# Mixture by pairs of experts, with rows turned by DMA, in a ViT layer on one core

## The reference

```
hidden = einsum('npd,hd->nph', patches, W_lin) + b_lin;  h = concat([cls, hidden])
q, k, v = heads(layernorm(h) @ qkv_weight.T)              # 12 heads of 16
q = layer_norm(q) * 16**-0.5;  k = layer_norm(k)
h = h + (softmax(q @ k.T) @ v) @ proj_weight.T
y = layernorm(h)                                          # 12608 rows of 192
scores = sigmoid(y @ gate_weight.T)                       # 8 experts
w, idx = top 2 experts of the 2 best groups of 4, by scores + gate_bias; w normalised
out_e = (silu(y @ w1[e].T) * (y @ w3[e].T)) @ w2[e].T     # 128 inner numbers
h = h + sum over idx of w * out_e + shared expert(y)
```

## Time and profile before

| what | us |
|---|---|
| median of 2 runs | 1719.84 (1719.72 to 1719.96) |
| profiled execution, its own time | 1721.13 |
| its span | 1719.3 |
| PE busy | 1622.7 (94%) |
| DVE busy | 1274.5 (74%) |
| ACT busy | 1010.0 (59%) |
| POOL busy | 602.2 (35%) |
| one attention step | 14.19 |
| one full mixture group | 29.69 |

### The profile page before, as it was taken

One profiled execution on the slowest core, in us unless ns is written; L12 is line 12 of the kernel. 1 busy time (PEld: TensorE's weight loads), 2 busy tenths in 40 slices (PEclk: granted clock), 3 DMA queues, 4 the chain that ended last, 5 costly groups with the idle time before them and its releaser, 6 DMA issues. The chain is left out here.

```text
span 1719.3 us, 44326 instructions
## 1 busy us (share of the span) xinstructions
PE 1622.7 (94%) x16914; PEld 1124.4 (65%) x16914; DVE 1274.5 (74%) x3660; ACT 1010.0 (59%) x2089; POOL 602.2 (35%) x658
## 2 busy tenths in 40 slices
PE   5999999999999999999998499999999999999998
PEld 4777777777777777777776255555555555555555
DVE  5677777666666666666664488888888888888887
ACT  2777776666666666666666345445454545455452
POOL 2333333333333333333331143343434343343433
PEclk8999999999999999999999699999999999999999
DMA  7233333333333333333310100001010100001000
GB/s 236 68 76 76 76 76 76 76 77 76 76 76 77 76 77 78 77 78 78 79 35 12 35 29 27 31 19 38 20 38 20 34 24 29 29 20 38 16 20 16
DMA packets 40863, 95.19 MB, mean 55 GB/s; under 512 B 4491, under 2 KB 17454, under 8 KB 40526
## 3 DMA queue, kind: packets, MB, share of 16 engines
q1 hardware_dynamic: 31438, 72.89, 13.6%
q0 software_dynamic: 9216, 19.47, 7.5%
HBM read 92.44 MB, written 19.37 MB: 65 GB/s over the span
## 5 line engine op out<-in xcount | busy, mean ns | idle before, releaser
L1343 POOL TENSOR_TENSOR in_lo<-inner,in_hi 128x512 f16<-128x512 f32 (+1 forms) x225 | 257.3, 1144 | 434.1 <-ACT act L1130 434.1
L885 POOL CAST qk_strips<-qk_norm 99x768 f16<-99x768 f32 x128 | 106.8, 835 | 606.3 <-DVE qk_norm L754 606.3
L589 ACT ACTIVATE prob<-ps_sc 99x792 f32<-99x792 f32 x384 | 302.5, 826 | 2.6 <-PE ps_sc L404 2.6
L1138 ACT ACTIVATE in_hi<-inner 128x512 f16<-128x512 f32 (+1 forms) x225 | 140.3, 624 | 181.2 <-DVE inner L1258 181.2
L1130 ACT ACTIVATE act<-ps_h 128x512 f32<-128x512 f32 (+1 forms) x225 | 131.7, 586 | 189.8 <-PE ps_h L1056 189.8
L1276 DVE SCALAR_TENSOR_TENSOR acc<-ps_y,comb,acc 128x192 f32<-128x192 f32 (+1 forms) x700 | 241.8, 407 | 0.3 <-PE ps_y L1072 0.3
L1258 DVE SCALAR_TENSOR_TENSOR inner<-ps_h,act 128x512 f32<-128x512 f32 (+1 forms) x225 | 153.6, 683 | 103.5 <-ACT act L1130 99.9
L1070 PE MATMUL ps_y<-w_hi,in_hi 128*128 128x192 f16 (+1 forms) x900 | 223.9, 249 | 3.7 <-DVE acc L1276 1.9
L1072 PE MATMUL ps_y<-w_hi,in_lo 128*128 128x192 f16 (+1 forms) x900 | 221.4, 246 | 0.0
L1071 PE MATMUL ps_y<-w_lo,in_hi 128*128 128x192 f16 (+1 forms) x900 | 221.4, 246 | 0.0
L342 PE MATMUL ps_hid<-lin_hi,x_hi 128*99 128x192 f16 x768 | 194.7, 254 | 18.9 <-DVE x_lo L701 10.4
(11 more groups left out here) (157 smaller groups left out, 3802.6 us busy)
## 6 DMA issues: line engine op xcount, KB each, us to landing
xin<-xp SPq DMA_DIRECT2D x64, 594.0 KB, 4.3
x_hi<-xp POOLq DMA_DIRECT2D x64, 297.0 KB, 4.0
hidden_dram<-h SPq DMA_DIRECT2D x64, 147.0 KB
hin<-hidden_dram SPq DMA_DIRECT2D x24, 384.0 KB, 3.1
out<-acc SPq DMA_DIRECT2D x24, 384.0 KB, 2.4
w_f<-w SPq DMA_DIRECT2D x1, 2304.0 KB, 9.2
hidden_dram<-h SPq DMA_DIRECT2D x64, 0.8 KB
w_f<-w SPq DMA_DIRECT2D x1, 864.0 KB, 11.2
```

The source lines that it names most:

```text
L589: act.activation(prob[quad][:, places].rearrange("p h m s -> p h (m s)"), ps_sc[0:TR, places, 0:2 * SLOTS], ACT.Exp, scale=D ** -0.5 / (SQ ...
L1343: pool.tensor_tensor(in_lo[b][:, 0:N], inner[b][:, 0:N], in_hi[b][:, 0:N], ALU.subtract).then_inc(inlo_done, 1)
```

## The change

1. Attention, DVE: `norm_hidden` is split by token half. The first half stays, then `o_out(n4, 0)` comes ahead of `qk_normalise(n2, 1)`, and the second half goes behind `v_copy`.
2. Mixture, all engines: the work goes by turns of two experts (`two_by_two`, across the border of groups). PE makes the 16 full-row products of both, then the four half-row products together (`inner_tails`), then the 24 outer-product matmuls of the two experts of the turn before. `inner`, `in_hi` and `in_lo` have four buffers in place of three.
3. Mixture, rows: ACT writes the normalised rows in float32, then their high half `y_hi` (with columns 128 to 191 a second time); POOL makes the remainder `y_lo`; SP turns both by DMA, 8 issues of 128x256 float16 for each group, two groups ahead (`transposes` on SP). PE's 8 transposes, ACT's and DVE's copies out of `ps_x` are gone.
4. The two PSUM banks of `ps_x` go to the outer products: `ps_y` is two by two banks. The router's product uses the free end of one of them, and PE waits for `tanh_done` before the older outer products of that turn.
5. POOL's `inner_rest` no longer waits for the next silu; DVE's router parts and statistics are spread over the turns.

```diff
@@ phase_a, DVE step
                 if n1.active():
-                    norm_hidden(n1)
-                if n2.active():
-                    qk_normalise(n2, 1)
-
+                    norm_hidden(n1, 0)
                 if n4.active():
                     o_out(n4, 0)
                 if n2.active():
+                    qk_normalise(n2, 1)
                     v_copy(n2)
+                if n1.active():
+                    norm_hidden(n1, 1)
@@ phase_b
+        def two_by_two(own_work, older_work):
+            turns = [(Index(0, g, 2, GROUPS_B), e) for g in range(GROUPS_B) for e in range(NE)]
+            for i in range(0, len(turns) + 2, 2):
+                own, older = turns[i:i + 2], turns[max(i - 2, 0):i]
+                own_work(own, lambda: [older_work(g, e) for g, e in older])
@@ SP
+            def transposes(g, half_no):
+                R, p = rows_of(g), g.mod(3)
+                sp.wait_ge(ylo_done, g.times(2, half_no + 1))
+                if half_no == 0 and reached(g.times(NE, -2 * NE)):
+                    sp.wait_ge(inner_done, g.times(NE, -2 * NE))
+                for t in (2 * half_no, 2 * half_no + 1):
+                    s = slice(t * R, (t + 1) * R)
+                    sp.dma_start_transpose(yT_hi[p][:, :, s], y_hi[0:R, t, :]).then_inc(yT_in[p], 16)
+                    sp.dma_start_transpose(yT_lo[p][:, :, s], y_lo[0:R, t, :]).then_inc(yT_in[p], 16)
@@ PE
+            def turn(own, older_products):
+                for g, e in own:
                     inner_products(g, e)
...
+                scored = [g.back(-1) for g, e in own if e == 3 and g.back(-1).active()]
+                for following in scored:
+                    g, e = own[0]
+                    if reached(g.times(2 * NE, 2 * e - 6)):
+                        pe.wait_ge(acc_done, g.times(2 * NE, 2 * e - 6))
+                    gate(following)
+                for g, e in own:
+                    inner_tails(g, e)
+                for following in scored:
+                    pe.wait_ge(tanh_done, following.times(1, 1))
+                older_products()
+            two_by_two(turn, outer_products)
@@ ACT
+            def turn(own, _):
+                for g, e in own:
+                    if e == 3 and g.back(-1).active():
+                        gate_out(g.back(-1))
+                for g, e in own:
                     silu(g, e)
+                for g, e in own:
                     inner_first(g, e)
...
+                for g, e in own:
+                    ahead = g.back(-2)
+                    if e == 5 and ahead.active():
+                        normalise(ahead, 0)
+                    if e == 6 + g.c % 2 and ahead.active():
+                        normalise(ahead, 1)
@@ DVE
+            def turn(own, older_sums):
+                for g, e in own:
                     multiply(g, e)
...
+                older_sums()
+                for g, e in own:
+                    following, ahead = g.back(-1), g.back(-2)
+                    if e == 0:
+                        route(g, 5)
+                    if e in (1, 2) and ahead.active():
+                        stats_of(ahead, e - 1)
+                    if e > 3 and following.active():
+                        route(following, e - 4)
@@ POOL
             def inner_rest(g, e):
...
-                if e + 1 < NE or g.back(-1).active():
-                    pool.wait_ge(silu_done, g.times(NE, e + 2))
+            def rest_of(g, half_no):
+                pool.wait_ge(yhi_done, g.times(2, half_no + 1))
+                pool.tensor_tensor(y_lo[0:R, ts, 0:C], bnorm[0:R, ts, :], y_hi[0:R, ts, 0:C], ALU.subtract)
+                pool.tensor_tensor(y_lo[0:R, ts, C:256], bnorm[0:R, ts, 128:C], y_hi[0:R, ts, C:256],
+                                   ALU.subtract).then_inc(ylo_done, 1)
...
                     inner_rest(g, e)
-                    if e == 5 and g.back(-2).active():
+                    if e == 3 and g.back(-2).active():
                         rstds(g.back(-2))
+                    if e == 6 and g.back(-2).active():
+                        rest_of(g.back(-2), 0)
+                    if e == 7 + g.c % 2 and g.back(-2).active():
+                        rest_of(g.back(-2), 1)
```

More of the change, by code:

```diff
@@ L726, in hidden_mean, with norm_hidden @@
                     dve.bn_aggr(meanvar[:, t, :], stats[:, t, :]).then_inc(mv_done, 1)
[L728 to L738, removed]
+            def norm_hidden(n, t):
+                if t == 0:
+                    dve.wait_ge(hrstd_done, n.times(1, 1))
+                    if reached(n.times(1)):
+                        dve.wait_ge(xT_done, n.times(1))
+                dve.tensor_scalar(xnorm[:, t, 0:C], h[n.mod(HB)][:, t, :], meanvar[:, t, 0:1],
+                                  h_rstd[:, t:t + 1], ALU.subtract, ALU.mult)
+                dve.tensor_scalar(xnorm[:, t, C:256], h[n.mod(HB)][:, t, 128:C], meanvar[:, t, 0:1],
+                                  h_rstd[:, t:t + 1], ALU.subtract, ALU.mult).then_inc(xnorm_done, 1)
             def xT_out(n):
@@ L915, in phase_b @@
         bshift = sb("bshift", [128, T])
-        bnorm = sb("bnorm", [128, T, 256])
-        yT_hi = [sb(f"yT_hi{p}", [128, 2, GT], F16) for p in range(2)]
-        yT_lo = [sb(f"yT_lo{p}", [128, 2, GT], F16) for p in range(2)]
+        bnorm = sb("bnorm", [128, T, C])
+        y_hi = sb("y_hi", [128, T, 256], F16)
+        y_lo = sb("y_lo", [128, T, 256], F16)
+        yT_hi = [sb(f"yT_hi{p}", [128, 2, GT], F16) for p in range(3)]
+        yT_lo = [sb(f"yT_lo{p}", [128, 2, GT], F16) for p in range(3)]
         act1 = [sb(f"act1{p}", [INTER, GT]) for p in range(2)]
-        inner = [sb(f"inner{p}", [INTER, GT]) for p in range(3)]
-        in_hi = [sb(f"in_hi{p}", [INTER, GT], F16) for p in range(3)]
-        in_lo = [sb(f"in_lo{p}", [INTER, GT], F16) for p in range(3)]
+        inner = [sb(f"inner{p}", [INTER, GT]) for p in range(4)]
+        in_hi = [sb(f"in_hi{p}", [INTER, GT], F16) for p in range(4)]
+        in_lo = [sb(f"in_lo{p}", [INTER, GT], F16) for p in range(4)]
         half = sb("half", [128, T, E])
@@ L1019, in transposes @@
                     s = slice(t * R, (t + 1) * R)
[L1020 to L1030, removed]
+                    dst = ps_gate[0:R, t * E:(t + 1) * E]
                     pe.matmul(dst, yT_hi[p][:, 0, s], gate_hi[:, 0], start=True, stop=False)
@@ L1075, in _ @@
             first = Index(0, 0, 2, GROUPS_B)
-            transposes(first)
             gate(first)
-            def body(g):
-                following = g.back(-1)
-                for e in range(NE):
+            def turn(own, older_products):
+                for g, e in own:
                     inner_products(g, e)
-                    if e > 1:
-                        outer_products(g, e - 2)
-                    elif g.back(1).active():
-                        outer_products(g.back(1), e + NE - 2)
-                    if e == 2 and following.active():
-                        transposes(following)
-                    if e == 4 and following.active():
-                        gate(following)
-                if not following.active():
-                    outer_products(g, NE - 2)
-                    outer_products(g, NE - 1)
-            run(body)
+                scored = [g.back(-1) for g, e in own if e == 3 and g.back(-1).active()]
[10 more added lines that the diff above has]
+            two_by_two(turn, outer_products)
         @block.scalar
@@ L1173, in stats_of @@
                     dve.bn_aggr(bmv[0:R, t, :], bstats[0:R, t, :]).then_inc(bmv_done, 1)
-            def yT_out(g):
-                N, p = T * rows_of(g), g.mod(2)
-                for k in range(2):
-                    dve.wait_ge(yThi_done, g.times(2, k + 1))
-                    dve.scalar_tensor_tensor(out=yT_lo[p][:, k, 0:N], in0=ps_x[k][:, 0:N], scalar=SX,
-                                             in1=yT_hi[p][:, k, 0:N], op0=ALU.mult,
-                                             op1=ALU.subtract).then_inc(yTlo_done, 1)
             ROUTE_STEPS = 19
@@ L1293, in _ @@
                 stats_of(second, half_no)
[L1294 to L1295 removed]
+            for part_no in range(5):
                 route(first, part_no)
[L1298 to L1300 removed]
+            def turn(own, older_sums):
+                for g, e in own:
                     multiply(g, e)
[L1302 to L1317 removed]
+                older_sums()
[7 more added lines that the diff above has]
+                        route(following, e - 4)
+            two_by_two(turn, accumulate)
         @block.gpsimd
```

152 lines of the change are left out of this document (71 added, 81 removed).

## The result

The changed kernel took **1694.78 us** (median of 2 runs, 1693.66 to 1695.89) against 1719.84: a ratio of 0.985, interval 0.9821 to 0.9879. It is faster, by 25 us where 54 were forecast; that is inside the range given, and less than the 2% that counted as faster. The profiled execution took 1693.66 us with a span of 1691.7.

The account below looks back on a forecast made before the run. PE's own row of instructions was taken to bound both phases. From the profiled 1721.1 us, minus 16 (attention), minus 41 (mixture), plus 3 (its start) gave 1667, as median 1666 us; range 1642 to 1750.

Parts of the forecast that it names:

- attention: Attention step: o_norm earlier shortens it by 0.26 us to 13.93, the fourth exponential then limiting; 16 us over 62 steps.
- mixture's groups, PE's own row: Mixture: dropped transposes and paired half-row products save PE a net 1.71 us a group, 41 us for 24 groups.
- DVE keeps up: Mixture: DVE, POOL and ACT all have room beside PE's shorter turns, so no time is lost to them.
- start of the mixture: First group's normalising, remainders and transposing DMAs take 8.4 us where 7.2 were; 3 us added, bounds 0 and 16.
- What bounds the kernel: Both phases: PE's own row of instructions sets the time; only what shortens it or makes it wait counts.
- Rival C: Attention: the exponential is not the limit, so the whole 40 us wait is gained; 1642 us, chance 0.07.
- What leaves PE: Mixture: a turn of two experts takes 6.09 us against 2 x 3.15; each half-row switch costs 0.21.
- DVE is the tight one ... It fits: Mixture: the fullest turn, with the router's five large steps, needs 5.98 of 6.09 us on DVE; 0.7 lateness free.
- Rival B: Mixture: DVE sets the turn, its operations or waits 5% longer, fullest turns 6.3 us; 1689 us, chance 0.10.
- The transposing DMAs: Mixture: at d = 0.6 us of SP's queue per DMA none stalls PE (up to 1.13); upper bound d 1.9.
- far side of rival A: Router's product: DMAs so late that PE stalls and the kernel slows by over 2%; d above 2.1 us, chance 0.13.
- The likeliest case: Whole kernel: the forecast of 1666 us itself, alone 1650 to 1684, d up to 1.3; chance 0.56.

Follow-up runs that it names:

- e1: The kernel before with the attention edit alone (DVE step order); 1702.47 us, ratio 0.9892 to the kernel before.
- e5: The changed kernel with POOL's y_lo remainders moved beside DVE's PSUM-reading work, in_lo behind them, ScalarE's normalisation one turn sooner; 1665.28 us, ratio 0.9675.
- e2: The changed kernel without POOL's y_lo remainders (one column still computed to keep the order of waits); 1664.75 us, ratio 0.9671.
- e8: The changed kernel without the attention edit, so the mixture edits alone; 1713.0 us, ratio 0.9948 to the kernel before.
- e10: The changed kernel with both e5's reordered remainders and e4's half-row products of each expert apart; 1689.11 us, ratio 0.9819.
- e4: The changed kernel with each expert's half-row products right behind its own full products, as before the change; 1692.57 us, ratio 0.9833.

## Why the prediction was wrong, step by step

Minus is time saved.

| term | forecast | measured |
|---|---|---|
| attention | -16 | -20 (starts of the mixture's load), -18.5 (e1) |
| mixture's groups, PE's own row | -41 | -45 (24 x 1.86, group 27.83 in e5) |
| DVE keeps up | 0 | +31 (e2), +30 (e5), up to 3 of it the late DMAs |
| start of the mixture | +3 | +7.4 (trace) |
| sum | -54 | -26.6 with e2's figure (medians: -25, spans: -27.6) |

**What bounds the kernel: right.** PE's own row did, and where it was freed of waits it is what sets the time.

**Attention: right.** 13.94 for 13.93 us, L388 without a wait, the scores held by the exponential, 0.29 us where 0.4 was forecast. Rival C is out. The 62 steps make 15.5 of the 20 us (62 x 0.25). The rest lies outside them and is not all the edit's: e8, whose attention is that of the kernel before, starts the mixture's load at 954.79 where the kernel before did at 958.66, so two executions of the same work differ by 3.9 us there.

**What leaves PE: right.** A turn took 6.08 us (forecast 6.09), and e10 measures the switches at 0.21 a turn. The group without stalls came out at 27.83, 0.15 better than forecast.

**"DVE is the tight one ... It fits": this is the step that failed.** The prediction gave the fullest turn 5.98 of 6.09 us with 0.7 of play, from durations in the kernel before. It had gone through POOL's load only as a sum (2.5 us more, over 12 free) and through DVE's only as a sum, and had not laid the two beside each other in time. The durations of DVE's small steps in the profile before are those with POOL elsewhere, and the change moved POOL's instructions on to them. The price is two turns of every nine, 7.24 in place of 6.08 us and 7.86 in place of 6.57, and over the kernel 30 us. The second of them is the turn that the prediction took for the fullest, with the five large steps: DVE lost 0.85 us there and as much in the turn ahead, more than the 0.7 of play. In the first, three blocked steps lost 1.84. The rule of the skill cited above was to be had; applied to each POOL instruction that moves, it would have asked which DVE instruction it now meets.

Rival B foresaw the place, L1061 waiting for `inner`, and 1689 us, but by another mechanism (DVE's operations with more PSUM banks, or longer waits between steps) and with a chance of 0.10. `acc` and `inner` kept their lengths, so its cause did not happen; its consequence did, that no merging of half rows is left (e4). That its 1689 lies 6 us from the measured time is luck: it takes the pairing away in every turn, where two turns of nine lose more than that and the others nothing.

**The transposing DMAs: price wrong, judgement nearly right.** One takes 1.29 us of SP's queue, twice the 0.6 taken and below the upper bound of 1.9. The prediction's own formula then gives 3d - 3.4 = 0.5 us in odd groups and none in even ones; measured are about 0.3, 11 times, 3.3 us in all. The far side of rival A is out. Neither bound had the mechanism. The pieces are somewhat more than the 256 that the upper bound counted, 88270 - 31438 = 56832 for 200 DMAs, 284 each, but short: 17.5% of 1691.7 less 13.6% of 1719.3 are 62 us of 16 engines, 0.0175 a piece where 0.119 was taken. What takes the time is SP's queue, held for 1.25 us by each issue. The page "VectorE: DVE Perf Modes" of the Trainium skill gives 1309 ns for 128x128; taken for a whole DMA that is what the trace shows, 1.29, though for 128x256, and taken for each of two tiles, as the prediction did, it is twice too much.

**Start of the mixture: mis-sized**, by the same d. With 1.29 in place of 0.6, and counted as it went, all eight of the first group one behind the other (949.00 to 958.05), the term is 7.4. The prediction had only three of them behind the second half, as if the first half's were through by then.

**The numbers.** The range held the result, but by luck: it was that wide for late DMAs, which took 3 us. The likeliest case's own range, 1650 to 1684, did not hold it. Most of the chance lay on faster by over 2%, and the result is 1.5%.

## What to carry to other kernels

Before work is moved on an engine, lay its new place beside the timelines of the other engines, not only beside their sums: a duration in a profile holds for the neighbours it had there. On DVE and POOL, put POOL's work beside DVE instructions that read PSUM, as e5 does. A gain on the fullest engine is worth what the next one can follow: make both edits, or measure the second one too, since alone the pairing measured as nothing (e4) and behind the cure as 23 us (e10).

## What the runs showed of the hardware

- A DVE instruction of 16 numbers in a row took up to 1.16 us in place of 0.17, ending within 0.05 us of the POOL instruction beside it, for `TENSOR_SCALAR` in float32 as well as for a `TENSOR_TENSOR` of 32 numbers (0.37 in place of 0.19); one of 256 numbers took 1.03 in place of 0.41. `SCALAR_TENSOR_TENSOR` with an operand in PSUM was not slowed.
- A transposing DMA of 128x256 float16 from SBUF to SBUF holds SP's queue for 1.25 us, 1.29 from issue to issue, and lands 2.4 us after its issue. A plain one (out) holds it for 0.33.
- Going to half-row products and back costs TensorE 0.21 us each time: a turn with two such visits takes 6.29 us, with one 6.08, for the same products.
